# Second chunk of a Mamba group on TensorE: skip products and output transposes ahead of the token products, state products directly behind them, second output projection behind the next group's first pair

## The reference, cut to what matters

```python
scores = einsum('bclhg,bcshg->bchls', Cc, Bc) * decay * dtT      # 128x128 for each head
Y_intra = einsum('bchls,bcshp->bclhp', scores, Xc)               # the token products
S = einsum('bcshg,bcshp->bchgp', Bc * w[..., None], Xc)          # what a chunk adds to the state
step: H = dlast * H + S                                          # state update, chunk after chunk
Y_inter = einsum('bclhg,bchgp->bclhp', Cc * exp(cum), Hprev)     # reads the state before the chunk
y = (Y_intra + Y_inter + D_skip[:, None] * Xc)                   # D_skip * Xc: the skip products
y = rmsnorm(y * silu(z), gnorm_w)
return y @ out_proj_w.T                                          # the output projection
x = x + layernorm(u + mixer(u))                                  # then the second block on x
```

## Time and profile before

| what | value |
|---|---|
| median of 3 runs | 2586.38 us |
| the profiled execution | 2586.19 us |
| its span, first to last instruction | 2584.5 us |
| mean granted TensorE clock over the span | 0.991 |
| TensorE matmul busy | 2504.1 us (97%) |
| VectorE / GpSimd / ScalarE busy | 83% / 81% / 70% |
| DMA queues, mean share | 4.2% |

### The profile page before, as it was taken

One profiled execution on the slowest core, in us unless ns is written; L12 is line 12 of the kernel. 1 busy time (PEld: TensorE's weight loads), 2 busy tenths in 40 slices (PEclk: granted clock), 3 DMA queues, 4 the chain that ended last, 5 costly groups with the idle time before them and its releaser, 6 DMA issues. The chain is left out here.

```text
span 2584.5 us, 59964 instructions
## 1 busy us (share of the span) xinstructions
PE 2504.1 (97%) x19384; PEld 1981.0 (77%) x19384; DVE 2149.3 (83%) x5557; ACT 1821.7 (70%) x3745; POOL 2082.8 (81%) x2939
## 2 busy tenths in 40 slices
PE   5899999999999999999999999999999999999987
PEld 3678777778777778777778777778778778778765
DVE  5678888888888888888888888888888888888887
ACT  4567777777777777777767777767777777777753
POOL 4478888888888888888888888888888888888875
PEclk8999999999999999999999999999999999999999
DMA  4000000000000000000000000000000000000000
GB/s 146 9 9 14 6 8 12 12 12 12 4 8 12 12 12 12 4 8 12 12 12 12 4 8 12 12 12 9 7 8 12 12 12 8 8 8 12 8 5 9
DMA packets 28861, 34.34 MB, mean 13 GB/s; under 512 B 2704, under 2 KB 27280, under 8 KB 28240
## 3 DMA queue, kind: packets, MB, share of 16 engines
q1 hardware_dynamic: 28816, 33.77, 4.2%
HBM read 25.37 MB, written 8.39 MB: 13 GB/s over the span
## 5 line engine op out<-in xcount | busy, mean ns | idle before, releaser
L1220 DVE SCALAR_TENSOR_TENSOR acc<-bank,cw,acc 128x253 f32<-128x253 f32 x1920 | 769.8, 470 | 100.0 <-ACT acc L840 98.4
L1619 PE MATMUL bank<-hT,w_in 128*128 128x256 f32 x2560 | 616.4, 384 | 14.0 <-DVE acc L1220 11.6
L1619 PEld LDWEIGHTS bank<-hT,w_in 128*128 128x128 f32 x2560 | 478.6, 191 | 129.7 <-issue 36.9
L628 POOL TENSOR_TENSOR Em<-ee 128x1024 f32<-128x1024 f32 x256 | 490.1, 1924 | 97.8 <-DVE rden L1356 95.2
L1376 DVE SCALAR_TENSOR_TENSOR Em<-Em,p 128x1024 f32<-128x1024 f32 x256 | 354.1, 1413 | 102.0 <-POOL Em L628 102.0
L643 POOL TENSOR_TENSOR W<-W,Em 128x1024 f32<-128x1024 f32 x124 | 294.8, 2378 | 52.7 <-ACT Em L975 44.5
L840 ACT ACTIVATE acc<-bank,cb,cw 128x253 f32<-128x253 f32 x640 | 324.0, 559 | 0.0
L975 ACT ACTIVATE Em<-Em,rden 128x1024 f32<-128x1024 f32 x256 | 289.9, 1145 | 47.8 <-DVE Em L1386 46.0
L1386 DVE TENSOR_TENSOR Em<-Em,products 128x1024 f32<-128x1024 f32 x248 | 297.4, 1210 | 0.0
L1820 PE MATMUL bank<-h2T,w_up 128*128 128x256 f32 x1024 | 245.0, 382 | 2.1 <-ACT hid L953 1.4
L1854 PE MATMUL bank<-w_ue,WT 128*128 128x256 f32 x1024 | 236.5, 384 | 0.5 <-ACT WT L985 0.5
(11 more groups left out here) (209 smaller groups left out, 4848.3 us busy)
## 6 DMA issues: line engine op xcount, KB each, us to landing
x_in<-x_dram SPq DMA_DIRECT2D x32, 256.0 KB, 2.7
x_res<-x_dram SPq DMA_DIRECT2D x32, 256.0 KB, 2.7
out_dram<-f SPq DMA_DIRECT2D x32, 256.0 KB, 2.2
w_in<-in_wT_dram SPq DMA_DIRECT2D x1, 1544.0 KB, 8.9
w_in<-in_wT_dram SPq DMA_DIRECT2D x1, 1024.0 KB, 5.6
w_up<-upT_dram SPq DMA_DIRECT2D x1, 1024.0 KB, 13.7
w_de<-down_eT_dram SPq DMA_DIRECT2D x1, 1024.0 KB, 15.6
w_down<-downT_dram SPq DMA_DIRECT2D x1, 1024.0 KB, 17.9
```

What stands on the lines that cost most here:

```text
L628: nc.gpsimd.tensor_tensor(Em[:, k], bc(ee[:, k, 0:XD], 2, KEYS), bc(ee[:, k, XD:XD + KEYS], 1, XD), ALU.mult).then_inc(E_done.sem, 1)
L1220: ins = V.scalar_tensor_tensor(acc[:, r, a, TAPS - 1:], ps[:, a * TOK + k:(a + 1) * TOK - TAPS + 1 + k], cw[:, t, k:k + 1], acc[:, r, a, T ...
L1619: last = mm(ring[j % 2][:, a * TOK:(a + 1) * TOK], w_in[:, k, at:at + P], hT[:, k, :], start=k == 0, stop=k == DK - 1)
```

## The change

`mixer_Yn` is split in three: `yb_free` (the wait for the PSUM bank), `mixer_Yn` (the token products) and `mixer_skip` (the skip products). Chunk 0 keeps its order. In chunk 1 the transposes of chunk 0 come between the skip products and the token products, S of chunk 1 directly behind the token products, the projection of chunk 0 ahead of the transposes of chunk 1. The projection of chunk 1 is issued in the next group, behind pair 0; for group 31 it is issued once behind the loop. No instruction of VectorE, ScalarE, GpSimd or SyncE is changed, no product is added or removed, and no DMA is moved.

```diff
-            def mixer_Yn(g, c, e, n):
+            def yb_free(g, c, e, n):
                 if c:
                     pe.wait_ge(Yn_read.sem, Yn_read.at(g, c - 1))
...
-                if c:
-                    pe.wait_ge(skips, INNER // P)
-                    for i in range(INNER // P):
-                        mm(yb[:, i * P:(i + 1) * P], xbcT[:, i, c * P:(c + 1) * P],
-                           skip[...], start=i == 0, stop=False)
+            def mixer_Yn(g, c):
                 pe.wait_ge(Xdt_done.sem, Xdt_done.at(g, c))
                 pe.wait_ge(sL_done.sem, sL_done.at(g, 2 * c + 1))
                 for h in range(HEADS):
...
+                if c:
+                    last.then_inc(Yn_ps.sem, 1)
+            def mixer_skip(g, c):
+                pe.wait_ge(skips, INNER // P)
+                for i in range(INNER // P):
+                    last = mm(yb[:, i * P:(i + 1) * P], xbcT[:, i, c * P:(c + 1) * P],
+                              skip[...], start=c > 0 and i == 0,
+                              stop=c == 0 and i == INNER // P - 1)
                 if c == 0:
...
+                    last.then_inc(Yn_ps.sem, 1)
@@ do_group
                 if a:
                     mixer_pair(g, 0)
+                if b:
+                    mixer_out(e, 1)
                 if c:
                     ffn_down(f, 0)
@@ end of do_group
-                    mixer_Yn(g, 0, e, n)
+                    yb_free(g, 0, e, n)
+                    mixer_Yn(g, 0)
+                    mixer_skip(g, 0)
                     mixer_B(g, 1)
                     mixer_Yi(g, 1)
                     mixer_scores(g, 1)
-                    mixer_Yn(g, 1, e, n)
+                    yb_free(g, 1, e, n)
+                    mixer_skip(g, 1)
                     mixer_yT(g, 0)
+                    mixer_Yn(g, 1)
                     mixer_S(g, 1)
+                    mixer_out(g, 0)
                     mixer_yT(g, 1)
-                    mixer_out(g, 0)
-                    mixer_out(g, 1)
@@ behind the last do_group
+            mixer_out(NG - 1, 1)
```

More of the change, by code:

```diff
@@ L1732, in mixer_Yn @@
                     pe.wait_ge(cum_sb.sem, cum_sb.at(g))
-                if c:
-                    pe.wait_ge(skips, INNER // P)
-                    for i in range(INNER // P):
-                        mm(yb[:, i * P:(i + 1) * P], xbcT[:, i, c * P:(c + 1) * P],
-                           skip[:, 2 * i:2 * i + 2, :].rearrange("p h d -> p (h d)"), start=i == 0, stop=False)
+            def mixer_Yn(g, c):
                 pe.wait_ge(Xdt_done.sem, Xdt_done.at(g, c))
@@ L1745, in mixer_Yn @@
                                   stop=c > 0 and h == HEADS - 1)
-                if c == 0:
[L1747 to L1752, removed]
+                if c:
[4 more added lines that the diff above has]
+                    last = mm(yb[:, i * P:(i + 1) * P], xbcT[:, i, c * P:(c + 1) * P],
+                              skip[:, 2 * i:2 * i + 2, :].rearrange("p h d -> p (h d)"), start=c > 0 and i == 0,
+                              stop=c == 0 and i == INNER // P - 1)
+                if c == 0:
+                    last.then_inc(Yn_ps.sem, 1)
             def mixer_yT(g, c):
```

## The result

The changed kernel took 2589.91 us (median of 16 runs) against 2586.21 us (16 runs) for the kernel before: ratio of the runs 1.0015, 95% interval 1.0008 to 1.0022. The forecast was 2589.5. One of the 16 runs of the changed kernel, at 2880 us with a granted clock of 0.847, was in a slower state and is left out of the ratio. So a change that takes 0.29 us of TensorE's own work out of each group, most of it array switching, made the kernel 0.15% slower.

The account below looks back on a forecast made before the run. TensorE, 97% busy, sets the 77.81 us period with a few short waits; 0.29 saved a group is eaten by a late chain at pair 3: 2586.2 + 3.5 - 0.2 = 2589.5 us, range 2582 to 2595.

Parts of the forecast that it names:

- The saving on TensorE: TensorE from skip products to `ffn_down`: 9.17 us in place of 9.46, 0.29 less a group, mostly array switching.
- The token products 0.38 later: Chunk 1's token products start 0.38 us later behind the skip products, delaying whatever waits for them without slack.
- the chain: Token products, VectorE's gate, ScalarE's square, GpSimd's queue to its root, VectorE's residual, pair 1's convolution, pair 3's load: +0.38 us.
- Slack of 0.27 at pair 3: Before the change, pair 3's weight load on TensorE was released 0.27 us before it would delay TensorE.
- 20.5 behind the skip products: Sign that the forecast is right: pair 3's products start 20.5 us behind the skip products in place of 20.37.
- The second sum on VectorE: VectorE's `tail_sum`, waiting for projection 1, comes 1.1 us later, as does the convolution of pair 0; price 0.
- the wait at pair 2: TensorE waits 0.06 us at pair 2 for VectorE's convolution of pair 0, inside the later wait at pair 3.
- Projection 0's cover: Projection 0 on TensorE waits between nothing and 0.1 us for ScalarE's copy of chunk 0's transposes.
- Sum: Whole run: 30 x 0.11 = +3.5 us (0.116 unrounded) over groups 2 to 31, less 0.2 in the ending: 2589.5 us.
- the ending: After the last group, `tail_sum` waits less for projection 1 but also needs a root: -0.2 us.
- Rival 2: GpSimd's root L570 falls beside a VectorE mask or residual, 0.92 us longer: 2617 us, milder 2592 to 2595; chance 0.16.

Follow-up runs that it names:

- after_short: Changed kernel with GpSimd's second expert collection of chunk 0 on 8 of 1024 columns, leaving out expert weights: period 77.68 us, 0.9982 of the kernel before.
- before_delay1: Kernel before with one more small GpSimd operation ahead of the third root: period 77.85 us, 2585.96 us (one run).
- before_delay2: Kernel before with two more small GpSimd operations ahead of the third root: period 78.03 or 78.16 us, 2593.3 us (one run).
- yn_first: Changed kernel, but token products and S before chunk 0's transposes, both projections in next group, VectorE's pair 0 convolution before tail_sum: 2576.68 us, 0.9965 of kernel before.
- after_conv0_first: Changed kernel with VectorE's convolution of pair 0 ahead of the sum waiting for projection 1: period 77.83 or 77.96 us, 2586.79 us (one run).
- yn_first_conv_old: yn_first with VectorE's order of the kernel before, the sum ahead of the convolution of pair 0: period 77.67 us, 2580.51 us (one run).
- before_out_late: Kernel before with only projection 1 moved behind the next group's pair 0: period 77.97 us, 2589.8 us (one run).
- after_root_early: Changed kernel with GpSimd's third root ahead of the second expert collection of chunk 0: period 78.10 us, 2592.15 us (one run).

## Why the prediction was right

- *The saving on TensorE*: predicted 0.29 a group, measured 9.46 - 9.17 = 0.29, and block by block the sum holds to 0.01 (token products 0.98, S 1.03, projection 0 1.83). The 0.10 at each side of half-array work could be taken from rows with other neighbours. Some 0.05 of the 0.29 is not switching but the wait for the last score tile, which the prediction names.
- *The token products 0.38 later*: 1243.60 - 1242.17 = 1.43 against 1.04, +0.39. The shift came through gate, square, GpSimd's queue and residual with 0.39 at each. after_short with its control shows the chain to be the cause: without one link 77.68, with it 77.93, and the same link removed where there is slack is worth 0.
- *Slack of 0.27 at pair 3*: before_delay1 (+0.31 in the chain) lengthened the period by 0.04, before_delay2 (+0.62) by 0.35 in the groups without the shorter wait; yn_first, which leaves the chain where it was, gained 0.27. One sign was put badly: pair 3's products were to start 20.5 behind the skip products, and they start at 20.38. The 20.5 had the 0.10 of a late first product in it, which shows only behind pair 3, at 22.21 in place of 22.10: +0.11, as forecast.
- *The second sum on VectorE*: +1.1 was predicted and +1.2 measured (9.53 behind the skip products in place of 8.32); the wait at pair 2, predicted as 0.06, is 0.17. The release behind the projection took 0.1 longer than I allowed. As forecast it hides in pair 3's wait (after_conv0_first). Had the chain had its slack, this would have been the price: 0.13 (yn_first_conv_old against yn_first) to 0.16 a group (before_out_late).
- *Projection 0's cover*: no wait, as in the better of the two cases.
- *Sum*: forecast 30 x 0.116 = 3.5 us, measured 3.4 over the 29 periods of the steady part (0.116 each) and 3.7 in the medians. The first groups and the ending (-0.2 in the forecast) cannot be checked against single profiles, since the granted clock differs there: 0.96 before and 0.94 after from 2430 us on. So it is the period that bears the forecast out; that the total came within 0.4 us of 2589.5, where totals of one kernel spread over 5 us, is in part luck.
- *Rival 2* (GpSimd and VectorE hold each other) did not happen in the changed kernel, since both moved by the same 0.39: L563 is 1.63 and L570 0.71 as before. It did happen in my own after_root_early, where they moved against each other.

One thing the prediction did not have: a second late release on GpSimd, in both kernels. S of chunk 0 waits for GpSimd's `Xw`; its load has an idle of 0.25 in place of 0.12. Some 8 us earlier the two small operations of GpSimd's `ffn_root` meet a VectorE mask that begins 0.05 us ahead of the first of them. In before_delay2, a group of 78.03 and one of 78.16:

```profile
763.04 0.23 POOL L584 TENSOR_SCALAR vf<-mvf 128x2 f32<-128x2 f32 x1
```

```profile
1075.31 1.32 POOL L584 TENSOR_SCALAR vf<-mvf 128x2 f32<-128x2 f32 x1
```

In the first the operation gets through and only the next one is held, to the mask's end (1.04 in place of 0.22). In the second it is held itself, and GpSimd is 0.28 later, of which 0.13 reach TensorE. Over 25 steady groups of each of the 14 profiles this tells the groups apart without exception: all 32 in which the operation gets through are 0.12 to 0.13 us shorter than the others of their kernel. In the kernel before and in the changed one it is held in every steady group, so the comparison of the two is not touched. No run moves the mask or the operation, so this rests on the rows alone, and why one comes through first is open.

## What to carry to other kernels

An engine at 97% busy is not alone in setting the time: look for its loads that are released by another engine, and take the slack from there. An edit that shortens the busy engine but delays what it *produces* takes from this slack twice, once by the saving and once by the delay; put the saving where the producer is not moved, as in yn_first. Before a queue is reordered, ask what the moved instruction will run beside and whether what it waits for is there. Where a period has two values, look for two instructions of two engines that start almost together.

## What the runs showed of the hardware

- A VectorE instruction from SBUF to SBUF and a GpSimd one can hold each other, and the one that comes second pays. The first instruction of L1293 takes 0.48 alone and 1.73 when it begins 0.9 into a collection, ending 0.29 behind it; the collection keeps its 2.35. GpSimd's L563 takes 0.70 alone and 1.63 when it begins 0.2 into a mask, ending 0.57 behind it; L597, which begins 0.13 ahead of a mask, takes 0.73. With 0.05 between the starts either came through first. So the loss is what is left of the other instruction and not a fixed price, and the 0.92 of rival 2 was one case of it. The Trainium skill says in "Advanced Engine Details and Errata", section "Mode Summary", that VectorE's second port is shared with GpSimd, and that GpSimd's instructions and those of VectorE that use two ports block each other. These rows agree as to the blocking; no run here shows whether these instructions use two ports.
- The period of 77.8 us repeats to 0.02, while totals of the same kernel spread over 5 us. An effect of 0.1 us a group can be read from one profile and not from one time, once the groups with the 0.13 above are told apart.
